# Attention and mixture-of-experts kernel: softmax reciprocals spread by transfers through DRAM, and the scores of all heads in a row

## The reference

```python
x = x + gnn(layernorm(x), adj, ...)
x = x + ffn(layernorm(x), ...)

# gnn: H = 4 heads of Dh = 32, keys in 8 chunks of 128, softmax inside each chunk
scores = einsum("bhnd,bhjcd->bhnjc", q, kc) / sqrt(Dh)
scores = clip(scores, -10, 10)
scores = where(mask == 0, -10, scores)
attn = softmax(scores, axis=-1)          # over the 128 keys of a chunk
ctx = einsum("bhnjc,bhjcd->bhnd", attn, vc)   # summed over the 8 chunks
out = ctx @ Wo.T + bo + x                # then a layer norm with gamma, beta
# ffn: 8 experts, the two best of each token, gelu between two products
```

## Time and profile before

| | us |
|---|---|
| median of 3 runs | 833.86 (832.61 to 836.44) |
| the profiled execution | 836.42, its span 834.6 |
| PE busy | 700.5 (84%) |
| DVE busy | 727.4 (87%) |
| ACT busy | 567.0 (68%) |
| POOL busy | 556.9 (67%) |
| steps of the attention (first clip to last) | 38.6 to 513.4 |

### The profile page before, as it was taken

The page is one execution under the profiler, slowest core; times in us unless marked ns, Lnnn a source line. Parts: engine busy times, 40 slices in busy tenths (PEclk is TensorE's granted clock), DMA queues, the critical chain, the costliest instruction groups (busy, mean ns, idle before and its releaser), DMA issues.

```text
span 834.6 us, 20579 instructions
## 1 busy us (share of the span) xinstructions
PE 700.5 (84%) x6443; PEld 366.1 (44%) x6443; DVE 727.4 (87%) x2032; ACT 567.0 (68%) x1091; POOL 556.9 (67%) x570
## 2 busy tenths in 40 slices
PE   4598699999999999999999898575620499999994
PEld 1322133333323233233333123464510499999994
DVE  4989999999999999999999999987661288888883
ACT  4596587897897987978978666534500377777772
POOL 1211557897887897987978999868777155555554
PEclk9789899999999999999999999555555599999998
DMA  8924503204105005013032001201111222222210
GB/s 281 241 56 118 130 2 88 66 1 126 28 26 127 2 27 126 3 55 98 1 102 52 1 2 38 65 27 30 40 53 53 54 66 71 80 76 77 66 49 2
DMA packets 47597, 54.37 MB, mean 65 GB/s; under 512 B 7668, under 2 KB 31313, under 8 KB 47490
## 3 DMA queue, kind: packets, MB, share of 16 engines
q10 hardware_dynamic: 12672, 23.07, 10.7%
q1 hardware_dynamic: 29858, 21.41, 9.6%
q0 software_dynamic: 4960, 8.58, 3.2%
HBM read 34.03 MB, written 20.75 MB: 66 GB/s over the span
## 4 chain that ended last, share of the span: by engine, by line
PE 43%; DVE 31%; POOL 12%; issue 10%; DMA 1%; ACT 1%; SPq 0%; POOLq 0%; DVEq 0%; ACTq 0%
PE score_ps L1494 8%; DVE rspread L999 7%; PE sum_ps L1508 7%; PE side_ps L1524 6%; POOL rows_dram L595 6%; DVE w L978 6%; DVE prob_ring L978 6%; PE score_ps L1452 3%; PE score_ps L1453 3%; PE score_ps L1454 3%; PE sum_ps L1734 2%; PE sum_ps L1740 2%; PE sum_ps L1736 2%; PE sum_ps L1738 2%; DVE prob_ring L988 2%
## 5 line engine op out<-in xcount | busy, mean ns | idle before, releaser
L1494 PE MATMUL score_ps<-stack_mem 128*128 128x512 f16 x512 | 158.3, 392 | 19.0 <-DVE prob_ring L978 13.4
L749 ACT ACTIVATE prob_ring<-prob_ring 128x1024 f32<-128x1024 f32 x128 | 134.2, 1054 | 49.3 <-DVE prob_ring L978 38.6
L535 POOL TENSOR_TENSOR ctx_sb<-ctx_sb,rspread 128x512 f32<-128x512 f32 x108 | 139.0, 1287 | 41.5 <-DVE rspread L999 32.5
L749 ACT ACTIVATE w<-w 128x1024 f32<-128x1024 f32 x128 | 134.2, 1055 | 33.1 <-DVE w L978 32.4
L978 DVE SCALAR_TENSOR_TENSOR w<-score_ps,limit 128x1024 f32<-128x1024 f32 x128 | 153.0, 1212 | 3.4 <-PE score_ps L1494 3.2
L978 DVE SCALAR_TENSOR_TENSOR prob_ring<-score_ps,limit 128x1024 f32<-128x1024 f32 x128 | 153.4, 1203 | 1.0 <-PE score_ps L1494 0.7
L602 POOL DMA_INDIRECT out_x<-xn,limit x91 | 89.7, 985 | 86.8 <-DVE xn L1349 71.1
L540 POOL TENSOR_TENSOR ctx_acc<-ctx_acc,ctx_sb 128x512 f32<-128x512 f32 x93 | 119.2, 1281 | 7.3
L1494 PEld LDWEIGHTS score_ps<-stack_mem 128*128 128x128 f16 x512 | 29.3, 97 | 183.0 <-issue 82.0
L872 ACT ACTIVATE xn<-score_ps,vec 128x128 f32<-128x128 f32 x364 | 99.1, 383 | 11.4 <-PE score_ps L1454 10.3
L999 DVE STREAM_SHUFFLE rspread<-prob_ring 128x256 f32<-128x256 f32 x256 | 101.5, 449 | 0.0
(11 more groups left out here) (236 smaller groups left out, 1591.1 us busy)
## 6 DMA issues: line engine op xcount, KB each, us to landing
stack_mem<-qk_dram ACTq DMA_DIRECT2D x56, 256.0 KB, 4.6
ctx_sb<-rows_dram SPq DMA_DIRECT2D x91, 66.5 KB, 1.9
qk_dram<-qk_hi ACTq DMA_DIRECT2D x16, 256.0 KB, 2.9
qk_dram<-qk_lo ACTq DMA_DIRECT2D x16, 256.0 KB, 4.1
x<-in_adj SPq DMA_DIRECT2D x4, 512.0 KB, 7.5
ctx_sb<-in_adj SPq DMA_DIRECT2D x4, 512.0 KB, 10.0
stack_mem<-qk_dram SPq DMA_DIRECT2D x16, 128.0 KB, 3.7
w<-in_L_ffn_W SPq DMA_DIRECT2D x4, 512.0 KB
```

The costliest lines, as they stand in the source:

```text
L535: pool.tensor_tensor(fresh, fresh, by, ALU.mult).then_inc(scaled_ready, 1)
L749: act.activation(prob_at(s, u), prob_at(s, u), ACT.Exp, scale=1.0 / SCORE).then_inc(exp_done, 1)
L1494: ins = pe.matmul(score_ps[:, h, :], kstack[:, par, h, k * P:k * P + P], qstack[:, par, h, half * HALF:half * HALF + HALF], start=True, st ...
```

## The change

For groups 0 to 13 (tiles 0 to 111) DVE's two shuffles of each tile go. In their place SP stores `rinv` (128x256 f32, 128 KB) into a DRAM tensor, waits for the landing, and loads each tile of `rspread` (128x512 f32, 256 KB) from it: four rows of 2 KB, each repeated over the 32 partitions of a head. The source is indexed head, repeat, column: 4 x 32 x 512. Each slot of the ring has its own semaphore, on which POOL waits. The sixteen tiles of the last batch (112 to 127) keep the shuffles. PE issues the scores of all four heads of a step in a row, and contexts and denominators behind each other; DVE clips both head pairs in a row, ahead of the step's other work. LAG becomes 13. The clearing of `rows_dram` moves on SP's queue to behind the loads of group 2. The two matmuls that put the bias into `wo` become one with 128 rows, both parts of the bias lying in one tile.

```diff
-    LAG = 12
+    LAG = 13
...
-            sp.wait_ge(consts_ready, CONSTS)
-            sp.wait_ge(stacked, 16 * STACKS * 2)
-            zeros_and_ones = gather[:, :, :].rearrange("p j d -> p (j d)")
-            for r in range(PAIRS + 1):
-                sp.dma_start(rows_dram[CAP * r:CAP * r + P, :], zeros_and_ones[:, 0:ROW]).then_inc(rows_begun, 16)
+            def begin_rows():
+
+                sp.wait_ge(consts_ready, CONSTS)
...
+            for G in range(LAST * STEPS // GROUP):
+                sp.wait_ge(rinv_ready, G + 1)
+                sp.dma_start(rinv_dram[G % 2], rinv[:]).then_inc(rinv_stored, 16)
+                sp.wait_ge(rinv_stored, 16 * (G + 1))
+                for j in range(GROUP):
+                    g = STARTS[G] + j
+                    wait(sp, chunk_added, g - SPREADS + 1)
+                    sp.dma_start(rspread[:, g % SPREADS, :],
+                                 rinv_dram[G % 2].rearrange("(h j c) n -> h j (c n)", h=HEADS, c=2)[:, j:j + 1, :]
+                                 .to_broadcast([HEADS, DH, HALF])).then_inc(rspread_loaded[g % SPREADS], 16)
+                if G == 2:
+                    begin_rows()
...
-                pool.wait_ge(rspread_ready, g + 1)
+                if b < LAST:
+                    pool.wait_ge(rspread_loaded[g % SPREADS], 16 * (g // SPREADS + 1))
+                else:
+                    pool.wait_ge(rspread_ready, s + 1)
...
-                wait(dve, rspread_ready, STARTS[G])
+                wait(dve, rinv_stored, 16 * min(G, LAST * STEPS // GROUP))
+                wait(dve, rspread_ready, STARTS[G] - STEPS * LAST)
...
                     clip(b, s, 0)
+                    clip(b, s, 1)
...
                         invert(STARTS.index(g - 2) - 1)
-                    clip(b, s, 1)
                     for n in due(g, GROUP + 2, SPREAD_BY):
-                        if last and n in STARTS[:-1] and n >= STEPS * LAST:
-                            invert(STARTS.index(n))
-                        spread(n // STEPS, n % STEPS)
+                        if n >= STEPS * LAST:
+                            if n in STARTS[:-1]:
+                                invert(STARTS.index(n))
+                            spread(n // STEPS, n % STEPS)
...
             def wo(n):
-                for i in range(2):
-                    pe.matmul(side_tiles(0), ones_row[0:1, :], bo_parts[:, i:i + 1, :].to_broadcast([1, TH, P]),
-                              start=(i == 0), stop=False)
+                pe.matmul(side_tiles(0), ones_row[:], bo_parts[:, :].rearrange("p (o d) -> p o d", o=1).to_broadcast([P, TH, P]),
+                          start=True, stop=False)
...
                     next_scores(s, 0)
+                    next_scores(s, 1)
...
                     if STEPS * b + s - DEPTH + 1 in STARTS:
                         old_denominators(s)
-                        next_scores(s, 1)
                         old_contexts(s)
                     else:
                         old_contexts(s)
-                        next_scores(s, 1)
                         old_denominators(s)
```

More of the change, by code:

```diff
@@ L95, in gnn_moe @@
         qk_bias = sb("qk_bias", [P, 2], F32)
-        bo_parts = sb("bo_parts", [1, 2, P], F16)
-        bo_sum = sb("bo_sum", [1, P], F32)
-        ones_row = sb("ones_row", [1, P], F16)
+        bo_parts = sb("bo_parts", [P, P], F16)
+        bo_high = sb("bo_high", [64, P], F16)
+        bo_sum = sb("bo_sum", [64, P], F32)
+        ones_row = sb("ones_row", [P, P], F16)
         unscale = sb("unscale", [P, P], F16)
@@ L226, in gnn_moe @@
         qk_dram = nc.dram_tensor("qk_dram", (4, P, N), F16, kind="Internal").ap()
+        rinv_dram = nc.dram_tensor("rinv_dram", (2, P, HALF // 2), F32, kind="Internal").ap()
         b2_dram = nc.dram_tensor("b2_dram", (2, E * E, 2 * P), F16, kind="Internal").ap()
@@ L273, in gnn_moe @@
         rspread_ready = sem("rspread_ready")
+        rinv_stored = sem("rinv_stored")
+        rspread_loaded = [sem(f"rspread_loaded{i}") for i in range(SPREADS)]
         scaled_ready = sem("scaled_ready")
@@ L417, in _ @@
             load_x(2)
-            sp.wait_ge(consts_ready, CONSTS)
-            sp.wait_ge(stacked, 16 * STACKS * 2)
-            zeros_and_ones = gather[:, :, :].rearrange("p j d -> p (j d)")
-            for r in range(PAIRS + 1):
-                sp.dma_start(rows_dram[CAP * r:CAP * r + P, :], zeros_and_ones[:, 0:ROW]).then_inc(rows_begun, 16)
+            def begin_rows():
+                sp.wait_ge(consts_ready, CONSTS)
+                zeros_and_ones = gather[:, :, :].rearrange("p j d -> p (j d)")
+                for r in range(PAIRS + 1):
+                    sp.dma_start(rows_dram[CAP * r:CAP * r + P, :], zeros_and_ones[:, 0:ROW]).then_inc(rows_begun, 16)
+            for G in range(LAST * STEPS // GROUP):
[10 more added lines that the diff above has]
+                    begin_rows()
             sp.wait_ge(ctx_done, STEPS * NB)
@@ L488, in _ @@
             pool.memset(neg_half[:], -0.5).then_inc(rstd2_ready, 1)
-            pool.memset(ones_row[:], 1.0).then_inc(bo_step, 1)
+            pool.memset(ones_row[:], 1.0)
+            pool.memset(bo_parts[:], 0.0).then_inc(bo_step, 1)
             pool.memset(unscale[:], 0.0).then_inc(consts_ready, 1)
@@ L1046, in _ @@
             dve.wait_ge(bo_done, 1)
-            dve.tensor_tensor(bo_sum[:], sum_ps[0:1, 0, 0:P], rows_bc[0:1, 0, :], ALU.add).then_inc(bo_step, 1)
+            dve.tensor_tensor(bo_sum[:], sum_ps[0:64, 0, 0:P], rows_bc[0:64, 0, :], ALU.add).then_inc(bo_step, 1)
             dve.wait_ge(bo_step, 2)
-            dve.tensor_copy(bo_parts[:, 0, :], bo_sum[:]).then_inc(bo_step, 1)
+            dve.tensor_copy(bo_high[:], bo_sum[:]).then_inc(bo_step, 1)
             dve.wait_ge(bo_step, 3)
-            dve.tensor_tensor(bo_parts[:, 1, :], bo_sum[:], bo_parts[:, 0, :], ALU.subtract).then_inc(bo_step, 1)
+            dve.tensor_copy(bo_parts[0:1, :], bo_high[0:1, :])
+            dve.tensor_tensor(bo_parts[32:33, :], bo_sum[32:33, :], bo_high[32:33, :], ALU.subtract).then_inc(bo_step, 1)
             copy_consts()
@@ L1358, in last_contexts @@
                 for s in range(first, STEPS):
-                    dve.wait_ge(rspread_ready, g + s + 1)
+                    dve.wait_ge(rspread_ready, s + 1)
                     dve.tensor_tensor(slots[s - first], slots[s - first], rspread[:, s % SPREADS, :], ALU.mult).then_inc(tail_step, 1)
@@ L1551, in _ @@
                 v_proj(0, c, c)
-            pe.matmul(sum_ps[0:1, 0, 0:P], bv_total[:], woT[:], start=True, stop=True).then_inc(bo_done, 1)
+            pe.matmul(sum_ps[0:64, 0, 0:P], bv_total[:].to_broadcast([P, 64]), woT[:], start=True, stop=True).then_inc(bo_done, 1)
             pe.wait_ge(mask_made, T)
```

## The result

The change made the kernel slower: 865.88 us (862.60 to 866.31, 4 runs) against 834.17 before in the same session, a ratio of 1.0367 with a 95% interval of [1.0348, 1.0386] (it is taken from all the runs, not from the two medians). The forecast was 812 us, 800 to 836.

The account below looks back on a forecast made before the run. PE and DVE were both taken as full, with four DMA engines the new bound. Gains of 18.0 us (batches 1 to 6) and 4.5 (first), less 1.0 (last), made 21.5: 812 us from 833.86, range 800 to 836.

Parts of the forecast that it names:

- PE's new order: PE's attention steps: fewer changes of matmul shape take a plain step from 3.08 to 2.84 us, 4.0 us a batch.
- DVE's batch of 47: DVE in a middle batch: 58.0 us busy less 11.0 for the 32 dropped shuffles gives 47.
- The reciprocal as no bound: DVE's 1.75 us reciprocal behind both clips: a 4.0 us step against PE's 2.84, two stalls of 0.3 us each.
- The first batch: First attention batch, 63.6 us and held up by DVE: 4.5 us gained, mainly from 12 dropped shuffles.
- the four engines' sum: DMA work on the loads' four engines in a middle batch: loads 43.0, existing transfers 8.3 to 12.8, stores 0.7 us.
- the 0.6 us of stalls: Middle batch: two stalls of 0.3 us from DVE's reciprocal, added with 0.2 for waits to 54.3, giving 55.1.
- rival B: Second group's chain of latencies to `wo` at s = 13: PE waits 2 us, batch 57.1, 824 us; chance 0.10.
- The clearing: 29 transfers on SP's queue between groups 2 and 3, with five steps for them: nothing, or 1 us once.
- The last batch: Last attention batch: POOL's later group 13 costs 4.9 us less 4.0 of slack, so about 1 us lost.
- A: Loads spread over 16 engines, 0.7 us each, hidden; batch PE's 53.6 + 0.6; 801 to 806 us; chance 0.18.
- C: Rows cost more than 0.084 us on the four engines; gain gone at 0.089 to 0.097; 887 us at 0.11; chance 0.17.
- D: The change of shape saves nothing on PE: batch stays at 57.6, time about 826 us; chance 0.05.

Follow-up runs that it names:

- e1: Changed kernel with each tile loaded in four transfers, one for each head, same bytes; ratio to the kernel before 0.9842.
- e2: Kernel before with only the new order on PE and DVE, shuffles kept; ratio to the kernel before 0.9983.
- e8: Changed kernel with each tile loaded in four transfers, one per head, and the old order of PE and DVE; ratio to the kernel before 1.0017.
- e6: Changed kernel with each tile loaded in four transfers and the clearing ahead of the first store; 816.12 us, ratio to the kernel before 0.9793.
- e7: Changed kernel with each tile loaded in two transfers of two heads, same bytes; ratio to the kernel before 1.3804.
- e10: Changed kernel whose loads bring only columns 0 to 255 of a tile, the other half set to 1 once; ratio to the kernel before 0.9818.
- e5: Changed kernel with the clearing of `rows_dram` ahead of the first store of reciprocals; ratio to the kernel before 1.0244.

## Why the prediction was wrong

**What held.** PE's new order: plain step 2.84 forecast, 2.83 measured; contexts ahead of denominators 0.86, measured 0.88. DVE's batch of 47: measured 47.9. The reciprocal as no bound, as far as e1 shows, where PE is busy 53.34 of 54.80 us. Four engines for the load, 0.084 us for a 2 KB row while loads alone are under way (24 GB/s an engine), and that these four engines become the bound. That the order gives nothing alone, and the relief of DVE less than both (e2, e8).

The first batch came out near its forecast (4.5 gained, 6.4 measured) by luck. In e6, where the loads are in time, it takes 62.9 us, a gain of 0.7 on 63.6. In the changed kernel POOL stood mostly idle while DVE took the roots, and the step with them took 8.0 us and not 13.7 (last section).

**The step that failed** is the size of the four engines' sum: "Sum 52.0 to 56.5 us a batch, the middle 54.3". Measured in the same terms it is 62.0: the loads 49.0 and not 43.0, the parts 12.2, near the upper end of their 8.3 to 12.8, the stores 0.8. The bound was named rightly, but it lies 8 us above PE's 53.6, not above it "by a little". The term that was mis-sized most is the row: "I take 0.084, because with 4 engines at work (100 GB/s) neither end is crowded as in those two rows". That holds only while loads are alone. Over four batches a row of a load took 783 us / 8192 = 0.096 on average, and 0.092 in e7. That the parts' rows on the same engines make the difference is likely, but no row here splits it up. Only the parts' term was given a crowded end, not the loads' own.

The second error is in the same line of the prediction, "I add the 0.6 us of stalls and 0.2 for waits between engines that are all near full: 55.1": it gives the others who share these engines no price. Each store or load of the parts has 128 partitions on one side and is done when the last of its rows is, and its last rows queue on the four full engines: 6.4 to 10.4 us for the store in place of 5.1, 11.0 for the last load in place of 4.5. That is how the full engines reach PE: from the fourth to the seventh batch it waits 15.9 us for the parts and 8.7 for ACT, while POOL waits 38.4 us for its own tiles, so the loads are late as well. The prediction had such a chain in rival B, but at `wo`. The three transfers cost 13 us more, of which some 8 came through to the batch (61.2 against e1's 53 to 55).

e1 takes away the crowding alone and the 8 us go. e10 leaves the four engines and halves what the loads put on them, 37.5 us of work in 54.0, and they go too; e7 puts all on two engines, and the batch follows their sum. What the runs do not show is how a batch rises between 37.5 us of work and 62, where waits of the chain might add to the sum.

**The clearing** was costed at "nothing, or 1 us once". It cost 10 us once (72.9 against 63.0 in e5). I had looked for who reads its result, at 550 us, and given it five steps; its 29 issues take 19.27 us, some 0.66 each, and what stood behind them on the queue was the next group's store.

**The last batch** was to lose 4.9 us by the end of POOL's tiles, of which 4.0 were slack. By tile 123 it lost 11.8. The premise was that POOL starts group 13 when its data is there, 17.0 us behind the first clip. The data was nearly there; POOL was not, for it was still at the tiles of group 12, whose loads had been late in the same way (23.2). Even in e6, whose batches are undisturbed, tile 103 ends 21.4 us behind the first clip, so 4.4 of the 6.2 us of error are the longer path itself, and 1.8 the crowding.

**The sum**, with the measured sizes in place of the forecast ones: batches 1 to 6 (counted from 0) took 380.0 us and 349.9 before, 30.1 more where 18.0 less were forecast, +48.1; the start of the attention and the first batch gave 2.3 + 1.9 more than thought, -4.2; the last batch cost 11.8 and not 4.9, +6.9. 814.9 + 48.1 - 4.2 + 6.9 = 865.7, against 865.9 measured.

**The rivals.** A was wrong of this kernel, but e6 makes its premise true. In e6's trace the last batch begins 28.6 us earlier than before (423.3 against 451.9), where A had 28; but 2.5 of it are the start and 0.7 the first batch, for which A had nothing and 4.5. By tile 123 10.1 of these are lost again (85.2 us behind the first clip against 75.1), where A had the last batch lose nothing more. The ratio leaves 17.3 us of gain [14.1 to 20.4]. B had a chain of latencies, with another place and 2 us a batch where some 8 were lost. C came nearest. Its formula, 512 t + 0.7 + 8.3 to 12.8, gives 62.1 us with t = 0.096 and the measured 12.2, and a batch took 61.7; it had put the end of all gain at t = 0.089 to 0.097. What it gave as causes, source rows read again and again or a shared port, is not what the rows show, for alone the loads move some 24 GB/s an engine on four engines and on two. And its example of 0.11 is too high: e7's loads alone would fill 16 x 64 x 0.11 = 113 us of a batch of 104.7. D is excluded by the rows of PE.

## What to carry to other kernels

A transfer confined to a few DMA engines is a cost for all others that use these engines. Add up what lies on those few, the other transfers' rows included, with a row's price as it is in company (here 0.092 to 0.096 us, alone 0.084), and compare the sum with the next bound: 62.0 against PE's 53.6 lost 8 us a batch, 37.5 lost nothing. Near full, every transfer with rows on these engines lands late, so look also at the longest chain of them. The average share of the engines does not show it (0.41 in the slow batch, 0.58 in the fast one). Look at the slowest dimension of both sides of a broadcast load, and cut it so that each piece spreads; and when a step is moved on a queue, count its issues against what then stands behind it.

## What the runs showed of the hardware

Small instructions of DVE slow down beside POOL. In the first batch of e6 the roots, 128x32 each, stand next to POOL's products; DVE's timeline, then POOL's:

```profile
91.10 0.19 DVE L951 SCALAR_TENSOR_TENSOR rstd<-msq,rstd 128x32 f32<-128x32 f32 x1
91.32 1.14 DVE L946 TENSOR_TENSOR msq<-rstd 128x32 f32<-128x32 f32 x1
92.49 0.19 DVE L948 SCALAR_TENSOR_TENSOR msq<-msq,var_e 128x32 f32<-128x32 f32 x1
92.72 1.17 DVE L951 SCALAR_TENSOR_TENSOR rstd<-msq,rstd 128x32 f32<-128x32 f32 x1
```

```profile
91.10 1.32 POOL L562 TENSOR_TENSOR ctx_acc<-ctx_acc,ctx_sb 128x512 f32<-128x512 f32 x1
92.58 1.26 POOL L557 TENSOR_TENSOR ctx_sb<-ctx_sb,rspread 128x512 f32<-128x512 f32 x1 [0.17 <-POOL ctx_acc L562]
```

L951 takes 0.19 us at 91.10, where it and POOL's instruction start together, and 1.17 behind one that POOL has already begun. The one of 1.14 us ends (92.46) just as POOL's ends (92.42), the next starts in POOL's gap and takes 0.19. Clips, whose source is PSUM, keep their 1.2 us beside the same work. The step of the roots has 19 such small instructions. It took 13.7 us in e6, where eight of them took 1.12 to 1.18 us, and 8.0 in the changed kernel, where POOL was idle more and two did. The Trainium skill (SBUF — State Buffer, "Who interferes with whom") has GpSimd and some forms of VectorE's instructions take one pair of ports in turn, each for its whole length; these rows agree.

A second one is the clock of PE behind a wait. The window that begins with the scores at 349.44, in the batch above:

```profile
349.40:351.40 2.00, 1.96 (x8) 0.58 (x12) 0.89 (x1) 0.94 (x1) 2.00 (x2) 0.50 0.30 111
```

PE had stood idle for 3.49 us, the granted clock is 0.50 of 2.4 GHz, and the scores take 1.89 us in place of 1.04. So this wait cost more than its length. Not every wait does: behind the 2.87 us before 340.88 the contexts took 1.06, as ever.
